# Expert stages in two groups of tokens, with the last batch's norms, routing and scatter between tiles of the first

## The reference, cut to what matters

```python
x = _layernorm(x + _L0_attn_ref(x, ...))
x = _layernorm(x + _L0_xattn_ref(x, ctx, ctx, ...))   # its own norm with gamma and beta inside
# experts, layer 0: 8 experts, F = 512, two per token
topk_values, topk_indices = jax.lax.top_k(einsum('bth,eh->bte', x, router_w), 2)
h1 = gelu(einsum('bth,efh->btef', x, w1) + b1)
expert_outputs = einsum('btef,ehf->bteh', h1, w2) + b2
mixed = sum(take_along_axis(expert_outputs, topk_indices) * softmax(topk_values))
x = _layernorm(x + mixed)
# layer 1: the same three; its experts have F = 256, relu, one expert per token
```

## Time and profile before

| | |
|---|---|
| median of 3 runs | 1644.38 us (1642.45 to 1647.92) |
| profiled execution | 1640.13 us, its span 1638.3 us |
| busy | PE 81%, DVE 52%, ACT 51%, POOL 33% of the span |
| the chain that ended last | PE 60%, DVE 19%, issue 8%, ACT 5%, DMA 5%, POOL 2% |
| first expert phase | first tile's transpose 843, last y about 928, phase D's first DVE work 952 us |
| second expert phase | first tile's transpose 1562, last y about 1600, end 1638 us |

### The profile page before, as it was taken

The page is one execution under the profiler, slowest core; times in us unless marked ns, Lnnn a source line. Parts: engine busy times, 40 slices in busy tenths (PEclk is TensorE's granted clock), DMA queues, the critical chain, the costliest instruction groups (busy, mean ns, idle before and its releaser), DMA issues.

```text
span 1638.3 us, 22200 instructions
## 1 busy us (share of the span) xinstructions
PE 1328.1 (81%) x6934; PEld 743.1 (45%) x6934; DVE 854.0 (52%) x2721; ACT 831.8 (51%) x1885; POOL 546.9 (33%) x511
## 2 busy tenths in 40 slices
PE   5999999999999888876549658788889897796460
PEld 2434434444443345444248636455555554444250
DVE  3444543453344354674522176777666775557525
ACT  4777677677677535453225345446454552343130
POOL 3455455455445411323454342100000110112253
PEclk9999999999999989987769879889999997887685
DMA  9000000000000000000259600000000000000172
GB/s 371 23 1 1 1 1 1 1 1 1 1 1 1 1 0 1 1 1 13 85 187 339 222 26 9 6 1 1 1 1 1 1 1 0 1 1 7 37 234 59
DMA packets 35074, 67.30 MB, mean 41 GB/s; under 512 B 5424, under 2 KB 21296, under 8 KB 33808
## 3 DMA queue, kind: packets, MB, share of 16 engines
q1 hardware_dynamic: 29328, 54.37, 9.6%
q0 software_dynamic: 5056, 10.36, 2.1%
q10 hardware_dynamic: 576, 1.16, 0.2%
HBM read 47.71 MB, written 18.15 MB: 40 GB/s over the span
## 4 chain that ended last, share of the span: by engine, by line
PE 60%; DVE 19%; issue 8%; ACT 5%; DMA 5%; POOL 2%; DVEq 0%; ACTq 0%; POOLq 0%
PE bank L503 8%; PE bank L485 7%; PE bank L493 6%; PE bank L432 5%; DMA work<-xs,xi 4%; PE bank L608 3%; PE bank L806 3%; PE bank L475 3%; PE bank L565 3%; PE bank L579 3%; PE bank L802 2%; DVE work L1321 2%; PE bank L594 1%; PE bank L672 1%; POOL xs L1866 1%
## 5 line engine op out<-in xcount | busy, mean ns | idle before, releaser
L1813 POOL TENSOR_TENSOR work<-work 128x512 f32<-128x512 f32 x256 | 266.5, 1041 | 277.6 <-DVE work L1329 277.6
L944 ACT ACTIVATE work<-bank,work 128x512 f32<-128x512 f32 x256 | 176.5, 689 | 117.8 <-DVE work L1321 117.6
L1321 DVE TENSOR_REDUCE work<-bank 128x1 f32<-128x512 f32 x256 | 176.7, 690 | 76.7 <-PE bank L485 75.8
L493 PEld LDWEIGHTS bank<-cst,work 128*128 128x128 f32 x1024 | 110.5, 140 | 164.4 <-issue 106.0
L493 PE MATMUL bank<-cst,work 128*128 128x128 f32 x1024 | 160.0, 283 | 6.6 <-ACT work L952 6.1
L1329 DVE RECIPROCAL work<-work 128x1 f32<-128x1 f32 x256 | 41.9, 164 | 222.6 <-ACT work L944 222.3
L952 ACT ACTIVATE work<-bank 128x512 f32<-128x512 f32 x256 | 152.6, 596 | 0.5 <-PE bank L493 0.5
L1914 POOL TENSOR_TENSOR work<-work 128x512 f32<-128x512 f32 x32 | 40.9, 1277 | 332.4 <-PE bank L806 312.6
L485 PE MATMUL bank<-work 64*128 64x512 f32 x512 | 144.5, 641 | 3.4 <-ACT work L944 3.4
L1853 POOL TENSOR_TENSOR work<-work 128x1232 f32<-128x1232 f32 (+1 forms) x32 | 55.5, 1735 | 250.3 <-DVE work L1401 250.2
L503 PE MATMUL bank<-work 128*64 128x512 f32 x512 | 137.4, 617 | 0.7 <-ACT work L952 0.7
(11 more groups left out here) (232 smaller groups left out, 2550.0 us busy)
## 6 DMA issues: line engine op xcount, KB each, us to landing
W<-in_wC SPq DMA_DIRECT2D x39, 578.0 KB
xs<-gat SPq DMA_DIRECT2D x9, 1024.0 KB, 16.5
W<-in_wF SPq DMA_DIRECT2D x23, 321.0 KB
ys<-work SPq DMA_DIRECT2D x62, 64.0 KB
x_all<-in_x SPq DMA_DIRECT2D x4, 256.0 KB, 8.7
W<-in_L_attn_Wq SPq DMA_DIRECT2D x2, 512.0 KB, 5.5
W<-in_L_attn_Wv SPq DMA_DIRECT2D x2, 512.0 KB, 7.6
W<-in_L_attn_Wo SPq DMA_DIRECT2D x2, 512.0 KB, 9.0
```

Source lines behind the costliest of these rows:

```text
L493: m = nc.tensor.transpose(out[:, k * P:(k + 1) * P], pA[u % 5][:, k * P:(k + 1) * P], ident)
L944: A(pA[u % 5], bank[u % 3][:, :], ACT.Exp, bias=nmax[:, u % 8:u % 8 + 1], accum_out=rsum[0][:, u % 8:u % 8 + 1]).then_inc(sem("a_e"), 1)
L1321: V.tensor_reduce(nmax[:, u % 8:u % 8 + 1], bank[u % 3][:, :], AX, ALU.max, negate=True)\
L1813: G.tensor_tensor(pA[u % 5], pA[u % 5], rsum[1][:, u % 8:u % 8 + 1].to_broadcast([P, S]), ALU.mult)\
```

## The change

The tokens are split in two groups, batches 0 to 2 and batch 3, each with its own `xs` and `ys` tensors, map and tiles. The number of tiles becomes 31 + 15 in C and 19 + 11 in F. The tiles of group 0 start when batches 0 to 2 are scattered. Batch 3's output projection still stands before the tiles; all else of it is put between tiles of group 0, at iterations named in `TAIL`, `STEPS` and `POOL_STEPS`. The gather buffers `xgM` go from three to six, `xTM` from two to three, and one iteration more lies between a tile's transpose and its matmuls. Batch 0's scatter is spread over u = 15 to 18. In C, batch 0's results are gathered between the gathers of tiles 41 to 44, and `close_x(0)` stands on DVE in iteration 46, ahead of the last three y additions. Result gathers wait only for their own group. In F, SP's weight load for tile 3 waits for batch 3's output projection. The core of the diff, in the order of the file:

```diff
+NG = 3
+CAPS = (NG * S, (NB - NG) * S)
+def tile_bound(k):
+    return [(k * c + E * (P - 1)) // P for c in CAPS]
+TILES0, TILES1 = tile_bound(2), tile_bound(1)
+NX = 6
...
-        xgM, a = carve(q_at, D, 3)
-        xTM, a = carve(a, P, 2)
+        xgM, a = carve(q_at, D, NX)
+        xTM, a = carve(a, P, 3)
...
-        TAIL = {0: (11, 16, 19, 19, 26), 1: (1, 3, 4, 5, 11), 2: (0, 1, 2, 3, 4), 3: (6, 7, 8, 8, 9),
-                4: (1, 3, 4, 5, 8), 5: (0, 1, 2, 2, 3)}
+        STEPS = {2: (13, 14, 15, 16, 17, 18, 19), 5: (7, 8, 9, 11, 12, 13, 14)}
+        POOL_STEPS = {2: (8, 21, 41), 5: (0, 15, 99)}
+        TAIL = {0: (11, 16, 19, 19, 26), 1: (1, 3, 4, 5, 11), 2: (0, 1, 5, 8, 12), 3: (6, 7, 8, 8, 9),
+                4: (1, 3, 4, 5, 8), 5: (0, 1, 4, 4, 6)}
...
+                    if m_["n"] == "F" and j == -m_["j0"] % NW:
+                        sp.wait_ge(y_ready, yn(PF))
...
             def moe(ph):            # PE
                 m_ = MOE[ph]
+                w, at = m_["w0"] - 1, STEPS[ph]
                 moe_logits(m_, 2)
-                tail(m_["w0"] - 1, 0)
                 moe_prefix(m_, 2)
-                for s in range(1, 5):
-                    tail(m_["w0"] - 1, s)
-                moe_logits(m_, 3)
-                moe_prefix(m_, 3)
-                n = m_["tiles"]
-                for j in range(n + 3):
+                tail(w, 0)
+                n = sum(m_["tiles"])
+                for j in range(n + 4):
                     if j < n:
                         moe_turn(m_, j)
-                    if 1 <= j <= n:
-                        moe_h(m_, j - 1)
-                    if j >= 3:
-                        moe_y(m_, j - 3)
+                    tail(w, j + 1)
+                    if j == at[0]:
+                        moe_logits(m_, 3)
+                    if j == at[3]:
+                        moe_prefix(m_, 3)
+                    if 2 <= j < n + 2:
+                        moe_h(m_, j - 2)
+                    if j >= 4:
+                        moe_y(m_, j - 4)
...
             def moe(ph):            # ACT
+                for j in range(n + 2):
+                    tail(w, j + 1)
+                    if j == at[1]:
+                        moe_exp(m_, 3)
...
             def moe(ph):            # DVE
                 moe_rank(m_, 2)
                 enter(dve, ph)
-                moe_map(m_)
+                moe_map(m_, 0)
+                moe_places(m_, 0)
+                for j in range(n + 4):
...
+                    tail(w, j + 1)
+                    if j == at[1]:
+                        moe_route1(m_, 3)
+                    if j == at[2]:
+                        moe_route2(m_, 3)
+                    if j == at[4]:
+                        moe_rank(m_, 3)
+                    if j == at[5]:
+                        moe_map(m_, 1)
+                    if j == at[6]:
+                        moe_places(m_, 1)
+                    if ph == 2 and j == n:
+                        close_x(m_, 0)
...
                     cross_tail(tail, c["w0"], u)
-                    if u == 15:
-                        moe_scatter(MOE[ph + 1], 0)
+                    if 15 <= u < 19:
+                        moe_scatter(MOE[ph + 1], 0, u - 15)
...
             def moe(ph):            # POOL
+                own, put, get = POOL_STEPS[ph]
+                for b in (1, 2):
+                    for t in range(NT):
+                        moe_scatter(m_, b, t)
                 enter(pool, ph)
+                for j in range(n):
+                    J = m_["j0"] + j
+                    if j == 0:
+                        pool.wait_ge(sem("M_xi"), m_["g0"] + 1)
+                        pool.wait_ge(sem("M_sc"), 16 * (done + NG * NT * K))
+                    if j == m_["tiles"][0]:
+                        pool.wait_ge(sem("M_xi"), m_["g0"] + 2)
+                        pool.wait_ge(sem("M_sc"), 16 * (done + NB * NT * K))
+                    if J >= NX:
+                        pool.wait_ge(sem("M_xtp"), J - NX + 1)
+                    rows_of = T["xs0" if j < m_["tiles"][0] else "xs1"]
+                    G.indirect_dma_start(xgM[J % NX], None, rows_of, bass.IndirectOffsetOnAxis(xi[:, j:j + 1], 0))\
+                        .then_inc(sem(f"M_x{J % NX}"), 16)
+                    if j == own:
+                        tail(m_["w0"] - 1, tail_steps(m_["w0"] - 1)[2])
+                    if put <= j < put + NT:
+                        moe_scatter(m_, 3, j - put)
+                    if get <= j < get + NT:
+                        moe_gather(m_, 0, j - get)
```

More of the change, by code:

```diff
@@ L299, in loaded @@
             eng.wait_ge(dma_in[what], 16 * n)
-        DMA_COUNT = {"x": 3, "small": 2, "late": 2, "A": 3, "B": 5, "D": 5, "E": 4, "zero": 10}
+        DMA_COUNT = {"x": 3, "small": 2, "late": 2, "A": 3, "B": 5, "D": 5, "E": 4, "zero": 11}
         ENDS = {0: [("a_pv", 32), ("a_o", 32)],
                 1: [("B_s", 16)],
-                2: [(f"M_ys{i}", 16 * len(range(i, TILES0, 3))) for i in range(3)],
+                2: [(f"M_ys{i}", 16 * len(range(i, sum(TILES0), 3))) for i in range(3)],
                 3: [("y_ready", 11), ("d_og", 32)],
@@ L1545, in moe_map @@
-                V.tensor_scalar(s2[:, 0:every], s2f[:, 0:every], -1.0, None, ALU.add).then_inc(sem("M_gi"), 1)
+                link(V.scalar_tensor_tensor(out=s2f[:, 0:every], in0=s2f[:, 0:every], scalar=float(P),
+                                            in1=rk[:, first:first + every], op0=ALU.mult, op1=ALU.add))
+                V.tensor_scalar(s2[:, first:first + every], s2f[:, 0:every], -1.0, None, ALU.add)\
+                    .then_inc(sem("M_gi"), 1)
             def moe(ph):
                 m_ = MOE[ph]
-                n, ft = m_["tiles"], m_["ft"]
+                w, at = m_["w0"] - 1, STEPS[ph]
@@ L1550, in moe @@
+                n, ft = sum(m_["tiles"]), m_["ft"]
                 moe_rank(m_, 1)
@@ new lines, in moe_scatter, with moe_gather @@
+            def moe_scatter(m_, b, t):
+                if t == 0:
+                    pool.wait_ge(sem("M_idx"), m_["b0"] + b + 1)
+                if m_["b0"] + b + t == 0:
+                    loaded(pool, "zero", DMA_COUNT["zero"])
+                for k in range(m_["k"]):
+                    G.indirect_dma_start(T[f"xs{group(b)}"], bass.IndirectOffsetOnAxis(s1[:, pair(m_, b, t, k)], 0),
+                                         x_all[:, 4 * b + t, :], None).then_inc(sem("M_sc"), 16)
+            def moe_gather(m_, b, t):
+                if t == 0:
+                    g = group(b)
+                    pool.wait_ge(sem("M_gi"), m_["g0"] + g + 1)
+                    for i in range(3):
+                        pool.wait_ge(sem(f"M_ys{i}"), 16 * len(range(i, last_tile(m_, g), 3)))
+                    if b >= 4 // m_["k"]:
+                        pool.wait_ge(sem("M_cb"), m_["b0"] + b - 1)
+                for k in range(m_["k"]):
+                    G.indirect_dma_start(gathered(m_, b, t, k), None, T[f"ys{group(b)}"],
+                                         bass.IndirectOffsetOnAxis(s2[:, pair(m_, b, t, k)], 0))\
+                        .then_inc(sem(f"M_g{b}"), 16)
@@ L1901, in phase_d @@
+                    if get <= j < get + NT:
+                        moe_gather(m_, 0, j - get)
+                if ph == 2:
+                    for t in range(NT):
+                        moe_gather(m_, 1, t)
+                else:
+                    for b in range(NB):
+                        for t in range(NT):
+                            moe_gather(m_, b, t)
             def phase_d():
@@ L1909, in phase_d @@
                     if g in (1, 5):
-                        moe_gather(MOE[2], 2 + g // 5)
+                        for t in range(NT):
+                            moe_gather(MOE[2], 2 + g // 5, t)
                     pool.wait_ge(sem("d_el"), g + 1)
```

205 lines of the change are left out of this document (96 added, 109 removed).

## The result

The changed kernel took 1675.32 us (median; 1673.24 to 1677.34) beside 1645.16 us of the kernel before: ratio 1.0183, 95% interval 1.016 to 1.0206. The forecast was 1609.7 us. It is 30 us slower where 35 us less were expected. The profiled execution spans 1675.5 us.

A forecast was written before the change was run, and what follows sets the result against it. The prediction saw idle chains ahead of and behind the tile loops, plus time per tile. Gains of 25.8 us through the first stage and 8.9 in the second made -34.7 us, from 1644.4 to 1609.7 us, range 1596 to 1628.

The forecast's parts named there:

- Step 4: First stage's tile loop: batch 3's work and other insertions between the tiles cost 8 us, from 3 to 11.
- Step 5: End of first stage: next phase begins 15.3 us after the last transpose, at 926.4, 25.8 us earlier than before.
- Step 6: Second stage: despite a PE stall of about 9 us ahead of tile 19, close_x(0) begins 8.9 us earlier in all.
- Rival (d): Tile loops: in-order engines let each hand-over of batch 3's chain hold all tiles; +54 us, 1663 us; chance 0.08.
- Step 1: End of cross-attention: spreading batch 0's scatters brings the last softmax normalisation 7.6 us sooner, 3.5 in the second stage.
- rival (c): Cross-attention: spread scatters don't release PE because ACT or DVE holds the last steps; price 11.1 us, 1621 us; chance 0.08.
- Step 2: Start of tiles: without batch 3 in the path, first transposes come 29.0 us earlier (814.3) and 18.4 in the second stage.
- Step 3: Tile loops: six buffers remove gather waits, giving 1.95 us a tile for 2.09, and 1.33 for 1.72 in the second stage.
- rival (a): Tile loops: DMA engines, not PE, set the pace, 2.12 and 1.72 us a tile; -21 us, 1623 us; chance 0.22.

The follow-up runs named there:

- g1: Kernel before with only batch 0's scatters spread over four steps of cross-attention: 1627.96 us (0.9964 of before), in a trickling set 1638.98 us (0.9969).
- e2: e1 plus eight gathers nobody reads, two behind each of tile gathers 36 to 39 of stage C: 1639.51 us, in a trickling set 1678.47 us.
- e3: e1 plus eight POOL memsets as long as e2's extra gathers, in their place: 1638.56 us, in a trickling set 1671.22 us.
- k1: e1 plus a short memset behind each of batch 3's scatters and tile gathers 21 to 30 of stage C: 1660.94 us (1.0157 of before).
- e1: Changed kernel with stage C's result gathers and close_x(0) put behind the tiles again: 1636.12 us, in a trickling set 1668.52 us.
- e4: e1 plus eight gathers nobody reads, one behind each of tile gathers 33 to 40 of stage C: 1637.10 us (1.0009 of before).
- h1: Changed kernel with the five loads of the next phase's weights behind the last tile's weights in SP's queue: 1678.13 us (1.0217 of before).
- e5: Changed kernel with stage F's result gathers held until its last tile's rows are written: 1634.59 us, +7.8 us.

## Why the prediction was wrong

The places in us, from the profiles of single executions (C0 and F0: first transposition of the stages; CL and FL: last; D: first DVE instruction of the next phase). The forecast's F0 and FL are shifted by its own -25.8.

| kernel | C0 | CL | D | F0 | FL | span |
|---|---|---|---|---|---|---|
| before | 843.4 | 922.4 | 952.2 | 1561.9 | 1596.6 | 1638.3 |
| forecast | 814.3 | 911.1 | 926.4 | 1517.7 | 1569.9 | 1603.6 |
| changed, no trickling | 823.1 | 927.0 | 944.2 | 1534.4 | 1590.5 | 1626.4 |
| changed, first profile | 821.8 | 954.5 | 971.6 | 1568.8 | 1631.3 | 1675.5 |
| g1, no trickling | 839.4 | 917.0 | 946.4 | 1558.4 | 1591.9 | 1631.5 |

**The sign: a cost that no term of the sum had.** What failed is in steps 4 to 6: they priced what is put between the tiles by the engine's own time and by lateness, and put at nothing what POOL's runs of DMAs do to the other engines. From the third line of the table to the fourth the first stage (C0 to CL) grows from 103.9 to 132.7 us, the second (F0 to FL) from 56.1 to 62.4, what is behind it from 35.9 to 44.3: 43 of the 49 us between the two profiles, all in stages with trickling. What in the kernel brings it on, in the sets that have it, is shown: POOL's indirect DMAs without gaps beside busy engines (e2 against e3, k1 against e1). That this is not enough is shown too: without trickling the changed kernel issues the same 20 in a row and e4 40, and nothing stalls. What in the chip couples them is not: in the trickling stretches the starts of PE's products lie 0.7, 1.4 or 2.1 us apart (939.83, 941.93, 944.03), which looks like instructions handed over one at a time, but no row shows by whom. A rival that no run tests is that the engines run out of instructions. The DMA packets that bring them are in the traces: in the first profile the last one ahead of the long stretch starts at 921.6 and the next at 950.9 (869.7 and 892.0 around the stretch of 876 to 886), while without trickling three start inside the run of 20 (912.5, 919.3 and 930.8). That fits engines that aren't fed as well as engines that use up nothing. Nor is it settled why some sets of runs have it and others not: the changed kernel's times within a set never mix the two, but one chip gave a set without trickling and later one with it, in which the executions of before lie in two groups (1633 to 1637 and 1641 to 1644). The kernel before is hardly touched (1642 to 1644 against 1636), probably because its long runs on POOL stand where the other engines do little: the earlier trace rows beside the earlier trace rows. I had taken POOL's dense runs in the earlier trace rows as harmless from exactly such places.

**Rival (d)** had the right sign and nearly the size (1663), but by luck: its mechanism is in-order hand-overs. Without trickling all that stands between the tiles cost 11 us over what was charged in the first stage (step 4 below), and the second stage came out 3.9 us over its forecast, not 35 together; the condition that it named for deciding was not met by hand-overs.

**The size without trickling: -9.0 us (-0.56%) for a forecast of -34.7.** By the steps, profile against profile:
- Step 1, 11.1 us forecast, measured by g1 alone 7.9 and 5.5 us between the medians (by the ratio of all executions 0.36% and 0.31%, which is 5 to 6 us). PE's idle 8.08 us for POOL are 0.39 now, but right behind them it waits 2.79 us for ACT (2.67 in g1): from the logits before it to the first product L637 (L608 before) 12.8 us pass in place of 18.0, 5.1 less and not 7.6. In the second stage 2.54 us for ACT stand in place of 3.49 for POOL, and it is 1.7 less, not 3.5. That ACT holds the last steps is rival (c), in part.
- Step 2, first stage: 823.1 for 814.3. Batch 1's scatters begin at 791.9, not 786.7: 2.1 of these 5.2 us are this execution's own (its logits at 765.30 stood at 763.16 before), 2.5 come from step 1. The landing takes 0.8 us more (5.53), and the first gather needs 5.6 us to its transposition for 2.54 in the earlier trace rows, 3.0 more. Tile weights and the next phase's weights, 6.8 MB, go out from 804.6 on, since SP waits for the last output projection, and DMA is full until 824; the prediction moved POOL's queue and not SP's against it. That these transfers are what delays the gather is not shown: h1 took 2.6 MB of them away and the gather still needed 5.3 us. The second stage's 18.4 us were near (F0 minus D: 590.2 for 609.6; 590 to 596 in the seven profiles of the changed kernel and its variants without trickling).
- Step 3: right on pace, 1.90 to 1.97 us a tile where undisturbed, so **rival (a)** falls. The DMA engines moved 417 GB/s from 816 to 820 and, in the first profile, 392 from 916 to 920, in the loop. The Trainium skill (DMA: Bandwidth & Descriptors, Specifications) has about 358 GB/s for one core, as half of what two cores share; here one core runs the whole program, and these rows are over it: the measurement decides. In the second stage it was 1.00 us a tile between waits, but POOL's 1.25 a gather, a weight that came 2.88 us late and lateness of the index (24.7 us behind F0 for 22.5) made 56.1 us out of 52.2.
- Step 4, charged 8 us: 19 over a pace of 1.90. Tiles 7 to 17 took 24.7 us for 19.0 (2.63 of them ahead of 842.41, for the gather behind POOL's own norm step, which the prediction let cost 1 us of the lead and nothing of the time; the rest hand-overs with DVE and PE's added work), tiles 17 to 25 took 24.0 for 15.2 (scatters; the wait of 3.07 at 877.12 is where it was expected, others lie around it), and tiles 31 to 45 took 30.7 for 26.6: result gathers put POOL's gathers 42 to 45 late, waits that the prediction did not list at all.
- Step 5: 17.2 us for 15.3; the last y waits 5.06 us for DVE behind close_x(0), as said.
- Step 6: the wait ahead of tile 19 was there (4.17 us, for 9 with the clock's loss); behind the last transposition 35.9 us for 33.7. e5 gives the overlap of result gathers as 7.8 us, about as priced.

(What step 3 of the prediction calls weights issues in the earlier trace rows are the puts of results, L384; its count of 31 tiles is right.)

The misses nearly all lie on one side. Each moved step was given its best place, and what the nearest row of before could not show (ACT behind the earlier normalisation, the first gather's 5.6 us, POOL's late gathers at the end) was taken as nothing or as the lower end.

## What to carry to other kernels

Price an engine's run of indirect DMAs by what stands beside it, not only by its own time: 12 to 20 in a row beside short instructions on the other engines cost 7 to 23 us in some sets of runs (tiles 17 to 25 with and without trickling, 30.6 against 24.0; the four tiles behind 923.95) and nothing in others. When a variant starts sooner, look first whether it was ahead before the place that was changed (here 2.1 of 4.0 us). A deeper buffer is also permission to issue without gaps. Before a change is judged, run it in more than one set, and ask of every queue that feeds the moved step (here SP's) what it is waiting for.

## What was not expected of the hardware

- The same program takes 1627 us in one set of runs and 1676 in another, each within 0.6%, by trickling of PE, ACT and DVE while POOL issues indirect DMAs 1.25 to 1.27 us apart; at 1.58 us apart PE did not trickle, in the one profile that has it. In the sets without trickling 20 and 40 such DMAs in a row changed nothing.
- DMA of one core at 392 to 417 GB/s over stretches of 4 us, and gapless tiles at 1.90 us with it.
